# Probabilities transposed one slot later in a fused attention and feed-forward kernel: five probability buffers, latent products in the fifth slot, other engines for the copies

## The chip, the cores and the metric

The kernel runs as one program on one core of a Trainium2 chip. The metric is the time of one execution on the device in microseconds (us). The engines are TensorE (PE in the profile, its weight loads PEld), VectorE (DVE), ScalarE (ACT), GpSimd (POOL) and SyncE (SP), which issues DMAs. Each engine works through its own queue of instructions; semaphores order the queues against one another.

## The reference

The input is 4 sequences of 512 rows of width 512. A block is a feed-forward layer with routed low-rank adapters, then attention, then the same feed-forward layer again. The change is in the attention, which is, cut to what matters:

```python
c_q = x @ w_q_down;  c_kv = x @ w_kv_down;  k_rope = rope(x @ w_k_rope)
q_lat  = einsum('bhsd,hdr->bhsr', q_nope, wuk)          # 32 heads, 64 latent values
scores = einsum('bhsr,btr->bhst', q_lat, c_kv) + einsum('bhsd,btd->bhst', q_rope, k_rope)
probs  = softmax(where(causal, scores / sqrt(192), min))
out_lat = einsum('bhst,btr->bhsr', probs, c_kv)         # the latent products
x = x + (einsum('bhsr,hdr->bhsd', out_lat, wuv) as [s, 4096]) @ w_out
```

## The kernel before

The four sequences are worked one after the other. In the attention of a sequence the 32 heads go in 16 pairs, and the causal score blocks of a pair are dealt to five units, each one PSUM bank of up to 512 columns (`MEMBERS`): units 0 and 1 are the last query block of either head (512 columns), units 2 and 3 are 384 + 128 columns, unit 4 is 256 + 256. So a sequence has 80 slots `u`, with `k = u % 5` the unit and `p = u // 5` the pair, and every engine has a hand-written queue that goes through the slots in this order. `known(g, u, n)` is true from slot n on.

In slot u, TensorE does, in this order: the three score products of unit u (lines L921 to L923, here s0 to s4); in slots k = 0 and 2 the five products that make the queries of one head of the next pair (L906, here q0 and q1); if `k == PV_SLOT`, the latent products of the pair before (`pv`, L957, 20 matmuls); the four transposes of the probabilities of slot `u - T_LAG` (L942, here T0 to T4); and in slots named by `OUT_SLOT`, from slot 15 on, one output row block (`output`, L983, six products).

The softmax of a unit runs over the others. VectorE masks the bank and takes its negated maximum (L1622), ScalarE takes exponentials into one of `RING` buffers `prob` and sums them (L1228), VectorE inverts the sums (L1576, one slot later), GpSimd multiplies (L631). After the transposes, the bank `probT_ps` (two of them, by turns) is copied to `probT` by ScalarE if the unit is in `ACT_BANKS` and else by VectorE (`copy_probT`, L390 and L392). `pv` waits until all five copies of its pair are done (`bank_copies`, with `ACT_COPIES` and `DVE_COPIES` counting them). VectorE also does the rotary part of the queries in slots k = 0 and 2 behind that slot's maximum: one product by the cosines (L1558) and two by the sines (L1563, L1564). It also adds the outputs (L1580) and takes the low part of `oT` (L1629).

Three places in the queues matter. VectorE takes the maximum of slot 3 only behind the rotary part of slot 2. ScalarE's exponential of slot u waits for that slot's maximum. And ScalarE's copy of a bank stands behind the exponential of its slot, except in slot k = 2, where it stands ahead of it:

```python
if copies and k == 2:
    copy_probT(act, nc.scalar, b, g, v)
...            # the exponential of slot u
if copies and k != 2:
    copy_probT(act, nc.scalar, b, g, v)
```

Of the kernel before, what the change touches and what calls it, by code (L numbers as in the profile page):

```python
# [26 lines left out]
F32 = mybir.dt.float32  # L27
# [7 lines left out]
P = 128  # L35
NB, S, D = 4, 512, 512
# [3 lines left out]
QL, KVL, DN, DR, DV = 192, 64, 128, 64, 128  # L40
# [11 lines left out]
STEPS = 3 * ST  # L52
# [17 lines left out]
    ((0, 1, 0), (1, 1, 256)),  # L70
)
RING = 4
T_LAG = 3
PV_SLOT = 3
HEAD_BLOCKS = 11
PT_BLOCKS = 2 * HEAD_BLOCKS
OUT_SLOT = {1: 0, 4: 1}
OUT_SLOT_TAIL = {1: 0, 2: 1}
TAIL = UNITS + 1
ACT_BANKS = (0, 2, 4)  # L80
SLOTS_OUT = 4
ACT_COPIES = (1, 1, 2, 2, 3)
DVE_COPIES = (0, 1, 1, 2, 2)


_INS = ["L0_attn_hidden_states", "L0_attn_w_q_down", "L0_attn_w_q_up_nope", "L0_attn_w_q_up_rope",
# [21 lines left out]
def build(nc, hidden, w_q_down, w_q_up_nope, w_q_up_rope, w_kv_down, w_k_rope, w_uk, w_uv, w_out,  # L108
          W_base, b_base, lora_A, lora_B, router_W, router_b, domain_prior, active,
          rope_cos, rope_sin, rope_cosT, rope_sinT, out):  # L110
    with ExitStack() as ctx:
# [8 lines left out]
        def place(name, shape, dt, at=None):  # L120
            size = int(np.prod(shape[1:])) * mybir.dt.size(dt)
            size = (size + 31) // 32 * 32
            where = cursor if at is None else at
            t = nc.alloc_sbuf_tensor_at(name, list(shape), dt, offset=where[0])
            where[0] += size
            assert where[0] <= sbuf_end, (name, where[0] - sbuf_end)
            return t
# [16 lines left out]
        sin_sb = place("sin_sb", [P, ST, 2, HALF], F32)  # L144
        ident = place("ident", [P, P], F32)
        mask = place("mask", [P, S], F32)
        small = place("small", [P, 60], F32)

        def columns(at, n):
            return small[:, at:at + n]  # L150
# [4 lines left out]
        neg_max = columns(28, 2 * RING).rearrange("p (r m) -> p r m", m=2)  # L155
        row_sum = columns(36, 2 * RING).rearrange("p (r m) -> p r m", m=2)
        inv_sum = columns(44, 2 * RING).rearrange("p (r m) -> p r m", m=2)
        ones, eps, minus_half = columns(52, 2), columns(54, 1), columns(55, 1)
        warm_slot = small[0:1, 56:60]
        region_a = [cursor[0]]  # L160
        wo_hi = place("wo_hi", [P, PAIRS, D], F32R)
        wo_lo = place("wo_lo", [P, PAIRS, D], F32R)
# [12 lines left out]
        rb = [region_b0]  # L175
# [16 lines left out]
        gate_row = place("gate_row", [1, 2 * NE], F32, rb)  # L192
        prior_raw = place("prior_raw", [P, NE], F32, rb)
        bias_nat = place("bias_nat", [P, KC], F32, rb)
        after_staging = rb[0]

        rb = [region_b0]
        prob = [place(f"prob{i}", [P, S], F32, rb) for i in range(RING)]
        probT = place("probT", [P, PT_BLOCKS, P], F32, rb)
        oT_hi = [place(f"oT_hi{i}", [P, S], F32R, rb) for i in range(3)]  # L200
        oT_lo = [place(f"oT_lo{i}", [P, S], F32R, rb) for i in range(3)]
        after_outputs = [rb[0]]
# [3 lines left out]
        moments = place("moments", [P, STEPS, 2], F32, after_outputs)  # L206
        var_eps, rough, newton, rstd = (place(n, [P, STEPS], F32, after_outputs) for n in
                                        ("var_eps", "rough", "newton", "rstd"))
        shift = place("shift", [P, STEPS], F32, [after_outputs[0]])

        uv_nat = [place(f"uv_nat{i}", [P, 2, KVL], F32, after_outputs) for i in range(SLOTS_OUT)]
        cosT = place("cosT", [P, S], F32, after_outputs)
        sinT = place("sinT", [P, S], F32, after_outputs)
        after_scores, turned_home = [after_outputs[0]], [after_outputs[0]]
# [13 lines left out]
        score_ps, probT_ps = X, Z  # L228
# [62 lines left out]
        inv_sum_set, prob_scaled, probT_done = sem("inv_sum_set"), sem("prob_scaled"), sem("probT_done")  # L291
# [55 lines left out]
        def known(g, u, least):  # L347

            return not isinstance(g, int) or BODY * g + u >= least
# [33 lines left out]
        def copy_probT(eng, do, b, g, v):  # L383

            pair = 16 * b + BODY_PAIRS * g + v // UNITS
            eng.wait_ge(probT_done, 80 * b + BODY * g + v + 1)
            if known(g, v, UNITS):
                eng.wait_ge(pv_done, pair)
            if eng.engine == nc.scalar.engine:
                do.activation(probT_unit(v), bank_unit(v), ACT.Copy).then_inc(probT_by_act, 1)  # L390
            else:
                do.tensor_copy(probT_unit(v), bank_unit(v)).then_inc(probT_by_dve, 1)  # L392
# [11 lines left out]
        with nc.Block() as block:  # L404
# [90 lines left out]
            def _(pool):  # L495
# [117 lines left out]
                def attend(b):  # L613
                    def work(g, u):
                        k, p = u % UNITS, u // UNITS
                        if k < 4 and within(g, u, UNITS * LAST_PAIR - 1):
                            m = q_index(b, BODY_PAIRS * g + p + 1, k // 2)
                            if k % 2:
                                qT_low(m, k // 2, (p + 1) % 2)
                            else:  # L620
                                if known(g, u, 1):
                                    pool.wait_ge(prob_scaled, 80 * b + BODY * g + u)
                                else:
                                    pool.wait_ge(qT_lo_set, m)
                                q_sum(m, k // 2, (p + 1) % 2)
                        if within(g, u, SLOTS - 1):
                            n = 80 * b + BODY * g + u
                            pool.wait_ge(inv_sum_set, n + 1)
                            for m, (_, i, c) in enumerate(MEMBERS[u % UNITS]):
                                w = (i + 1) * P  # L630
                                last = nc.gpsimd.tensor_tensor(prob[u % RING][:, c:c + w], prob[u % RING][:, c:c + w],  # L631
                                                               inv_sum[:, u % RING, m:m + 1].broadcast_to([P, w]),
                                                               ALU.mult)
                            last.then_inc(prob_scaled, 1)
                    attention(work, 0)
# [9 lines left out]
            def _(pe):  # L645
# [285 lines left out]
                def transpose_probs(b, g, v):  # L931
                    pe.wait_ge(prob_scaled, 80 * b + BODY * g + v + 1)
                    if known(g, v, 2):
                        by_act, by_dve = bank_copies(b, g, v - 2)
                        if (v - 2) % UNITS in ACT_BANKS:
                            pe.wait_ge(probT_by_act, by_act)
                        else:
                            pe.wait_ge(probT_by_dve, by_dve)
                    for h, i, c in MEMBERS[v % UNITS]:
                        for j in range(i + 1):  # L940
                            at = slice(c + j * P, c + (j + 1) * P)
                            last = nc.tensor.transpose(probT_ps[v % 2][:, at], prob[v % RING][:, at], ident[:])  # L942
                    last.then_inc(probT_done, 1)

                def pv(b, g, p):
# [58 lines left out]
                def attend(b):  # L1004
                    def work(g, u):
# [11 lines left out]
                        if k == PV_SLOT and known(g, u, UNITS):  # L1017
                            pv(b, g, p - 1)
                        if known(g, u, T_LAG) and within(g, u, SLOTS - 1 + T_LAG):
                            transpose_probs(b, g, u - T_LAG)  # L1020
                        if output_rows(u) is not None and known(g, u, 3 * UNITS):
# [12 lines left out]
            def _(act):  # L1034
# [173 lines left out]
                def attend(b):  # L1208
                    def work(g, u):
                        k, p = u % UNITS, u // UNITS  # L1210
                        n1 = BODY_PAIRS * g + p + 1
                        queries = within(g, u, UNITS * LAST_PAIR - 1)
                        if k == 0 and known(g, u, 2 * UNITS):
                            oT_high(b, g, p)
                        if k in (2, 4) and queries:
                            qT_high(q_index(b, n1, k // 2 - 1), k // 2 - 1, (p + 1) % 2)
                        v = u - T_LAG
                        copies = known(g, u, T_LAG) and within(g, u, SLOTS - 1 + T_LAG) and v % UNITS in ACT_BANKS
                        if copies and k == 2:
                            copy_probT(act, nc.scalar, b, g, v)  # L1220
                        if within(g, u, SLOTS - 1):
                            n = 80 * b + BODY * g + u
                            act.wait_ge(neg_max_set, n + 1)
                            if known(g, u, RING):
                                act.wait_ge(probT_done, n - RING + 1)
                            for m, (_, i, c) in enumerate(MEMBERS[k]):
                                w = (i + 1) * P
                                last = nc.scalar.activation(prob[u % RING][:, c:c + w], score_ps[u % 2][:, c:c + w],  # L1228
                                                            ACT.Exp, bias=neg_max[:, u % RING, m:m + 1], scale=-1.0,
                                                            accum_out=row_sum[:, u % RING, m:m + 1])  # L1230
                            last.then_inc(prob_set, 1)
                        if copies and k != 2:
                            copy_probT(act, nc.scalar, b, g, v)
                    attention(work, TAIL)

# [8 lines left out]
            def _(dve):  # L1244
# [363 lines left out]
                def attend(b, more):  # L1608
                    def work(g, u):
# [21 lines left out]
                        if k in (0, 2) and queries:  # L1631
                            if not known(g, u, UNITS):
                                dve.wait_ge(x_moved[k // 2], 32 * b + 1)
                            q_rotary(q_index(b, n1, k // 2), k // 2, (p + 1) % 2, qT_ps[k // 2])
                        v = u - T_LAG
                        if known(g, u, T_LAG) and within(g, u, SLOTS - 1 + T_LAG) and v % UNITS not in ACT_BANKS:
# [34 lines left out]
```

## Time and profile before

| | |
|---|---|
| median of 3 runs | 1167.78 us (1166.98 to 1170.35) |
| profiled execution | 1167.57 us |
| its span, first to last instruction | 1165.8 us |
| busy, share of the span | PE 95%, DVE 78%, POOL 63%, ACT 54% |
| mean granted TensorE clock | 0.992 |

The span is 1.8 us shorter than the time of the same execution. PE's busy time is modelled from pipelined matmuls, so in a list of its instructions the distance from one start to the next is what tells the cost; a duration includes the tail that overlaps the next instruction. A row with an idle time says so in brackets, with what ended it.

### The profile page before, as it was taken

Reading aid. Unit: us, or ns where it says so; the run is one execution under the profiler, and the core shown is the slowest. Engines: PE = TensorE matmul, PEld = TensorE weight load, DVE = VectorE, ACT = ScalarE, POOL = GpSimd, SP = SyncE. Lnnn points to the kernel's source line nnn. Section 1 sums busy time; section 2 is a strip of 40 time slices with the busy share of each in tenths; the row PEclk is TensorE's granted clock in tenths of the full one; section 3 lists DMA queues with packets and bytes.
Section 4 is the critical chain, followed back from the end, with each engine's and each line's share of the span. In section 5 each row is a group of like instructions: output and inputs, shape, how many; then the busy total and the mean of one; then the engine's idle time right before and its main releaser. Section 6 shows DMA issues by size and latency. Waiting matters only on the chain.

```text
span 1165.8 us, 21866 instructions
## 1 busy us (share of the span) xinstructions
PE 1105.7 (95%) x7284; PEld 906.6 (78%) x7284; DVE 908.2 (78%) x2667; ACT 623.9 (54%) x1733; POOL 740.0 (63%) x951
## 2 busy tenths in 40 slices
PE   5896999999998999999999899999999899999997
PEld 4755788888797788888788678888888678888876
DVE  4767888888676888878776888788867787888855
ACT  3554655555454655555535555655545466555542
POOL 2406977887432978787631887787723598877841
PEclk9998999999999999999999999999999999999998
DMA  9660000000101000000101000000010100000000
GB/s 286 179 194 1 1 1 1 1 1 1 37 10 64 2 1 2 1 1 1 37 1 37 37 2 1 2 1 2 1 37 28 47 1 1 1 1 2 1 1 37
DMA packets 22248, 30.96 MB, mean 27 GB/s; under 512 B 9302, under 2 KB 11094, under 8 KB 21498
## 3 DMA queue, kind: packets, MB, share of 16 engines
q1 hardware_dynamic: 19770, 24.85, 6.7%
q10 hardware_dynamic: 2368, 4.72, 1.2%
q8 instruction: 59, 0.97, 0.3%
q14 instruction: 51, 0.42, 0.1%
HBM read 22.23 MB, written 4.19 MB: 23 GB/s over the span
## 4 chain that ended last, share of the span: by engine, by line
PE 79%; DVE 7%; POOL 7%; ACT 3%; issue 2%; SPq 1%; DMA 1%; POOLq 0%; DVEq 0%
PE Y L983 15%; PE Y L957 12%; PE XZ L942 11%; PE Y L906 10%; PE XZ L922 6%; PE XZ L923 6%; PE XZ L921 5%; PE Y L675 4%; POOL prob L631 3%; PE XZ L675 2%; POOL qT_lo L542 2%; PE XZ L650 2%; POOL q_sums L537 2%; DVE xT_lo L1281 1%; ACT xT_hi L1037 1%
## 5 line engine op out<-in xcount | busy, mean ns | idle before, releaser
L1228 ACT ACTIVATE prob<-XZ,small 128x512 f32<-128x512 f32 (+3 forms) x512 | 266.3, 525 | 282.8 <-DVE small L1622 282.8
L631 POOL TENSOR_TENSOR prob<-prob,small 128x512 f32<-128x512 f32 (+3 forms) x512 | 360.7, 721 | 50.1 <-DVE small L1576 40.4
L1622 DVE CUSTOM_DVE_ANT_0 XZ<-XZ,mask 128x512 f32<-128x512 f32 (+3 forms) x512 | 247.9, 506 | 114.6 <-PE XZ L923 110.5
L537 POOL TENSOR_TENSOR q_sums<-q_sums,q_turned 64x512 f32<-64x512 f32 (+2 forms) x130 | 164.2, 1263 | 201.5 <-DVE q_turned L1564 200.1
L942 PE MATMUL XZ<-ident,prob 128*128 128x128 f32 x1280 | 196.3, 276 | 3.2 <-POOL prob L631 2.9
L921 PE MATMUL XZ<-kT_hi,qT_hi 128*128 128x512 f32 (+3 forms) x512 | 176.9, 345 | 12.7 <-ACT prob L1228 6.8
L542 POOL TENSOR_TENSOR qT_lo<-q_sums,qT_hi 128x512 fp32r<-128x512 f32 (+2 forms) x130 | 165.2, 1271 | 31.9 <-ACT qT_hi L1195 31.8
L942 PEld LDWEIGHTS XZ<-ident,prob 128*128 128x128 f32 x1280 | 149.5, 140 | 43.2 <-POOL prob L631 10.6
L922 PE MATMUL XZ<-kT_lo,qT_hi 128*128 128x512 f32 (+3 forms) x512 | 165.4, 323 | 0.0
L923 PE MATMUL XZ<-kT_hi,qT_lo 128*128 128x512 f32 (+3 forms) x512 | 165.2, 323 | 0.0
L957 PE MATMUL Y<-probT,ckv 128*64 128x384 f32 (+2 forms) x1280 | 152.3, 384 | 0.0
L390 ACT ACTIVATE probT<-XZ 128x512 f32<-128x512 f32 x192 | 114.9, 598 | 66.0 <-PE XZ L942 64.8
L957 PEld LDWEIGHTS Y<-probT,ckv 128*64 128x64 f32 x1280 | 81.8, 136 | 60.7 <-issue 47.3
L921 PEld LDWEIGHTS XZ<-kT_hi,qT_hi 128*128 128x128 f32 x512 | 97.2, 190 | 22.8 <-issue 7.7
L983 PE MATMUL Y<-wo_hi,oT_hi 128*128 128x512 f32 x256 | 110.9, 433 | 1.5 <-DVE x_sb L1580 1.4
L1580 DVE TENSOR_TENSOR x_sb<-Y,x_sb 128x512 f32<-128x512 f32 x128 | 87.8, 686 | 29.4 <-PE Y L983 29.1
L1228 ACT ACTIVATION_READ_ACCUMULATOR prob<-XZ,small 128x1 f32 x512 | 101.9, 199 | 0.0
L923 PEld LDWEIGHTS XZ<-kT_hi,qT_lo 128*128 128x128 f32 x512 | 97.3, 190 | 5.5
L922 PEld LDWEIGHTS XZ<-kT_lo,qT_hi 128*128 128x128 f32 x512 | 97.7, 191 | 4.8
L983 PE MATMUL Y<-wo_hi,oT_lo 128*128 128x512 f32 x256 | 101.1, 395 | 0.0
L983 PE MATMUL Y<-wo_lo,oT_hi 128*128 128x512 f32 x256 | 100.2, 391 | 0.0
L1195 ACT ACTIVATE qT_hi<-q_sums 128x512 fp32r<-128x512 f32 (+2 forms) x130 | 80.2, 617 | 19.0 <-POOL q_sums L537 19.0
(220 smaller groups left out, 2162.0 us busy)
## 6 DMA issues: line engine op xcount, KB each, us to landing
wout_nat<-in_L_attn_w_out_dram SPq DMA_DIRECT2D x16, 512.0 KB, 5.0
out_dram<-x_sb SPq DMA_DIRECT2D x16, 256.0 KB, 2.0
x_next<-_attn_hidden_states_dram SPq DMA_DIRECT2D x12, 256.0 KB, 3.4
x_sb<-x_next SPq DMA_DIRECT2D x12, 256.0 KB, 2.3
wbase_nat<-in_L_ffn_W_base_dram ACTq DMA_DIRECT2D x1, 1024.0 KB, 5.7
x_sb<-_attn_hidden_states_dram ACTq DMA_DIRECT2D x4, 256.0 KB, 7.0
nope_a<-_L_attn_w_q_up_nope_dram ACTq DMA_DIRECT2D x1, 1024.0 KB, 5.4
rope_a<-_L_attn_w_q_up_rope_dram SPq DMA_DIRECT2D x1, 1024.0 KB, 8.0
```

The costliest lines, as they stand in the source:

```text
L537: nc.gpsimd.tensor_tensor(q, q, turned, ALU.add).then_inc(q_sum_set, 1)
L542: nc.gpsimd.tensor_tensor(qT_lo[par][:, head, cols], q_sums[par][:, head, cols], f32(qT_hi[par][:, head, cols]), ALU.subtract).then_inc(qT ...
L631: last = nc.gpsimd.tensor_tensor(prob[u % RING][:, c:c + w], prob[u % RING][:, c:c + w], inv_sum[:, u % RING, m:m + 1].broadcast_to([P, w] ...
L906: last = nc.tensor.matmul(bank[:, cols], w, c, start=(j == 0), stop=(j == 4))
L921: nc.tensor.matmul(bank[:, c:c + w], high, kT_hi[:, 0:w], start=True, stop=False)
L922: nc.tensor.matmul(bank[:, c:c + w], high, kT_lo[:, 0:w], start=False, stop=False)
L923: last = nc.tensor.matmul(bank[:, c:c + w], low, kT_hi[:, 0:w], start=False, stop=True)
L942: last = nc.tensor.transpose(probT_ps[v % 2][:, at], prob[v % RING][:, at], ident[:])
L957: last = nc.tensor.matmul(o_ps[64 * h:64 * h + 64, column * P:(column + n) * P], ckv[:, j, :], probT[:, HEAD_BLOCKS * h + at:HEAD_BLOCKS * ...
L983: last = nc.tensor.matmul(bank, o[buffer][:, rows], w, start=(k == 0 and j == 0), stop=(k == 1 and j == 2))
L1228: last = nc.scalar.activation(prob[u % RING][:, c:c + w], score_ps[u % 2][:, c:c + w], ACT.Exp, bias=neg_max[:, u % RING, m:m + 1], scale= ...
L1622: last = nc.vector.tensor_tensor_reduce(bank, bank, mask[:, S - w:S], -1.0, HIGHEST, ALU.add, ALU.min, neg_max[:, u % RING, m:m + 1])
```

## The change

Transposes stand four slots behind the scores instead of three, with a fifth `prob` buffer for it. The latent products move from slot 3 to slot 4, the second output row block from slot 4 to slot 3. ScalarE now copies units 1, 3 and 4, VectorE 0 and 2; each still has as many copies as before, in the same slots. ScalarE's copy stands behind the exponential in every slot. Some small arrays (`shift`, `uv_nat`, constants) get other places in SBUF to make room.

```diff
 RING = 4
-T_LAG = 3
-PV_SLOT = 3
+PROBS = 5
+T_LAG = 4
+PV_SLOT = 4
-OUT_SLOT = {1: 0, 4: 1}
+OUT_SLOT = {1: 0, 3: 1}
 OUT_SLOT_TAIL = {1: 0, 2: 1}
-ACT_BANKS = (0, 2, 4)
+ACT_BANKS = (1, 3, 4)
-ACT_COPIES = (1, 1, 2, 2, 3)
-DVE_COPIES = (0, 1, 1, 2, 2)
+ACT_COPIES = (0, 1, 1, 2, 3)
+DVE_COPIES = (1, 1, 2, 2, 2)
...
-        prob = [place(f"prob{i}", [P, S], F32, rb) for i in range(RING)]
+        prob = [place(f"prob{i}", [P, S], F32, rb) for i in range(PROBS)]
...
-                            last = nc.tensor.transpose(probT_ps[v % 2][:, at], prob[v % RING][:, at], ident[:])
+                            last = nc.tensor.transpose(probT_ps[v % 2][:, at], prob[v % PROBS][:, at], ident[:])
...
                         copies = known(g, u, T_LAG) and within(g, u, SLOTS - 1 + T_LAG) and v % UNITS in ACT_BANKS
-                        if copies and k == 2:
-                            copy_probT(act, nc.scalar, b, g, v)
                         if within(g, u, SLOTS - 1):
                             n = 80 * b + BODY * g + u
                             act.wait_ge(neg_max_set, n + 1)
-                            if known(g, u, RING):
-                                act.wait_ge(probT_done, n - RING + 1)
+                            if known(g, u, PROBS):
+                                act.wait_ge(probT_done, n - PROBS + 1)
...
-                        if copies and k != 2:
+                        if copies:
                             copy_probT(act, nc.scalar, b, g, v)
```

On TensorE, in a pair in the middle of a sequence, these are the rows before, from the transposes T4 of slot 2 through the scores s3 (384 and 128 columns) to the latent products (the number behind a name is that of its buffer):

```order
L942 MATMUL XZ<-ident,prob_104 128x128 x4
L921 MATMUL XZ<-kT_hi,qT_hi_127 128x384
L922 MATMUL XZ<-kT_lo,qT_hi_127 128x384
L923 MATMUL XZ<-kT_hi,qT_lo_129 128x384
L921 MATMUL XZ<-kT_hi,qT_hi_127 128x128
L922 MATMUL XZ<-kT_lo,qT_hi_127 128x128
L923 MATMUL XZ<-kT_hi,qT_lo_129 128x128
L957 MATMUL Y<-probT,ckv 64x384 x2
L957 MATMUL Y<-probT,ckv 64x128 x2
L957 MATMUL Y<-probT,ckv 64x384 x2
```

Only the scores s3 stand between T4 and the latent products that need its copy. Now the same transposes T4 stand in slot 3, behind s3 (of which the last rows are shown), and an output row block and the scores s4 follow:

```order
L923 MATMUL XZ<-kT_hi,qT_lo_129 128x128
L942 MATMUL XZ<-ident,prob_111 128x128 x4
L983 MATMUL Y<-wo_hi,oT_hi_114 128x512
L983 MATMUL Y<-wo_lo,oT_hi_114 128x512
L983 MATMUL Y<-wo_hi,oT_lo_117 128x512
L983 MATMUL Y<-wo_hi,oT_hi_115 128x512
L983 MATMUL Y<-wo_lo,oT_hi_115 128x512
L983 MATMUL Y<-wo_hi,oT_lo_118 128x512
L921 MATMUL XZ<-kT_hi,qT_hi_127 128x256
```

The latent products come behind the six scores of 256 columns, and then T0:

```order
L921 MATMUL XZ<-kT_hi,qT_hi_127 128x256
L922 MATMUL XZ<-kT_lo,qT_hi_127 128x256
L923 MATMUL XZ<-kT_hi,qT_lo_129 128x256
L957 MATMUL Y<-probT,ckv 64x384 x2
L957 MATMUL Y<-probT,ckv 64x128 x2
L957 MATMUL Y<-probT,ckv 64x384 x2
L957 MATMUL Y<-probT,ckv 64x256 x2
L957 MATMUL Y<-probT,ckv 64x128 x2
L942 MATMUL XZ<-ident,prob_107 128x128 x4
```

So one output and one unit of scores more stand between T4 and the latent products, and the same instructions otherwise.

On ScalarE, before, the copy of T4 (the one that writes `probT` as 128x2x2x128) stands ahead of the exponentials of slots 2 and 3:

```order
L1195 ACTIVATE qT_hi_127<-q_sums_133 128x512
L390 ACTIVATE probT<-XZ 128x2x2x128
L1228 ACTIVATE prob_106,small<-XZ,small 128x384
L1228 ACTIVATE prob_106,small<-XZ,small 128x128
L1228 ACTIVATE prob_103,small<-XZ,small 128x384
L1228 ACTIVATE prob_103,small<-XZ,small 128x128
L390 ACTIVATE probT<-XZ 128x4x128
```

Now it stands behind both:

```order
L1195 ACTIVATE qT_hi_127<-q_sums_133 128x512
L1226 ACTIVATE prob_109,small<-XZ,small 128x384
L1226 ACTIVATE prob_109,small<-XZ,small 128x128
L390 ACTIVATE probT<-XZ 128x4x128
L1226 ACTIVATE prob_110,small<-XZ,small 128x384
L1226 ACTIVATE prob_110,small<-XZ,small 128x128
L390 ACTIVATE probT<-XZ 128x2x2x128
L1195 ACTIVATE qT_hi_127<-q_sums_133 128x512
```

What moved: the copy of T4 from ahead of the exponential of slot 2 to behind that of slot 3, and the other two copies name other units.

## Rows read from the trace of the kernel before

**Rows 1.** The page, busy time, share of the span and instructions of each engine:

```profile
PE 1105.7 (95%) x7284; PEld 906.6 (78%) x7284; DVE 908.2 (78%) x2667; ACT 623.9 (54%) x1733; POOL 740.0 (63%) x951
```

**Rows 2.** Windows: length, busy of PE, PEld, DVE, ACT, POOL, granted clock, DMA:

```profile
80.00:96.00 16.00, 10.26 (x59) 6.91 (x57) 10.65 (x31) 5.97 (x17) 4.43 (x5) 0.92 0.03 7
...
370.00:389.00 19.00, 15.19 (x81) 11.58 (x80) 16.91 (x47) 9.74 (x27) 15.43 (x17) 1.00 0.15 56
...
413.00:562.00 149.00, 149.00 (x952) 121.91 (x952) 124.83 (x355) 86.65 (x245) 118.14 (x134) 1.00 0.00 1
```

**Rows 3.** Timeline, TensorE, latent products of sequence 1 (start, us, engine, line):

```profile
389.24 2.38 PE L957 MATMUL Y<-probT,ckv 128*64 128x384 f32 x20
...
413.25 2.38 PE L957 MATMUL Y<-probT,ckv 128*64 128x384 f32 x20
...
561.67 2.38 PE L957 MATMUL Y<-probT,ckv 128*64 128x384 f32 x20
...
583.34 2.38 PE L957 MATMUL Y<-probT,ckv 128*64 128x384 f32 x20
```

**Rows 4.** The transposes by line: what ended TensorE's waits before them:

```profile
  POOL prob L631: 13.5, 31
```

**Rows 5.** Timeline, TensorE, one pair, pv to pv:

```profile
480.71 2.38 PE L957 MATMUL Y<-probT,ckv 128*64 128x384 f32 x20
483.02 0.66 PE L942 MATMUL XZ<-ident,prob 128*128 128x128 f32 x4
483.44 0.36 PE L921 MATMUL XZ<-kT_hi,qT_hi 128*128 128x256 f32 x1
...
484.23 0.60 PE L942 MATMUL XZ<-ident,prob 128*128 128x128 f32 x4
...
486.06 0.39 PE L921 MATMUL XZ<-kT_hi,qT_hi 128*128 128x512 f32 x1
...
488.25 0.48 PE L921 MATMUL XZ<-kT_hi,qT_hi 128*128 128x512 f32 x1
...
489.39 0.47 PE L983 MATMUL Y<-wo_hi,oT_hi 128*128 128x512 f32 x1
...
490.86 0.34 PE L921 MATMUL XZ<-kT_hi,qT_hi 128*128 128x384 f32 x1
...
492.87 0.60 PE L942 MATMUL XZ<-ident,prob 128*128 128x128 f32 x4
493.22 0.42 PE L921 MATMUL XZ<-kT_hi,qT_hi 128*128 128x384 f32 x1
...
494.21 2.38 PE L957 MATMUL Y<-probT,ckv 128*64 128x384 f32 x20
```

**Rows 6.** Timeline, ScalarE, the same pair: copy of T4; copy behind exponential of slot 3:

```profile
480.01 0.60 ACT L390 ACTIVATE probT<-XZ 128x512 f32<-128x512 f32 x1 [1.02 <-PE XZ L942]
...
483.72 0.60 ACT L390 ACTIVATE probT<-XZ 128x512 f32<-128x512 f32 x1
```

**Rows 7.** Timeline, VectorE, the same pair: maxima of slots 3, 0, 3, rotary part between:

```profile
481.75 0.57 DVE L1622 CUSTOM_DVE_ANT_0 XZ<-XZ,mask 128x384 f32<-128x384 f32 x1
...
486.94 0.70 DVE L1622 CUSTOM_DVE_ANT_0 XZ<-XZ,mask 128x512 f32<-128x512 f32 x1
...
493.13 0.67 DVE L1558 TENSOR_TENSOR q_sums<-Y,cosT 128x512 f32<-128x512 f32 x1
...
495.25 0.57 DVE L1622 CUSTOM_DVE_ANT_0 XZ<-XZ,mask 128x384 f32<-128x384 f32 x1
```

**Rows 8.** Timeline, VectorE, second and third pair of sequence 1:

```profile
388.11 0.69 DVE L1558 TENSOR_TENSOR q_sums<-Y,cosT 128x512 f32<-128x512 f32 x1
...
394.35 0.69 DVE L1622 CUSTOM_DVE_ANT_0 XZ<-XZ,mask 128x512 f32<-128x512 f32 x1
...
395.41 0.69 DVE L1629 TENSOR_TENSOR oT_lo<-Y,oT_hi 128x512 fp32r<-128x512 f32 x1 [0.29 <-ACT oT_hi L1206]
...
400.32 0.68 DVE L1558 TENSOR_TENSOR q_sums<-Y,cosT 128x512 f32<-128x512 f32 x1
```

More of the change, by code:

```diff
@@ L146, in build @@
         mask = place("mask", [P, S], F32)
-        small = place("small", [P, 60], F32)
+        small = place("small", [P, 64], F32)
         def columns(at, n):
@@ L157, in build @@
         inv_sum = columns(44, 2 * RING).rearrange("p (r m) -> p r m", m=2)
-        ones, eps, minus_half = columns(52, 2), columns(54, 1), columns(55, 1)
-        warm_slot = small[0:1, 56:60]
+        ones, eps, minus_half, warm_slot = columns(5, 2), columns(3, 1), columns(4, 1), small[0:1, 2:3]
+        shift = columns(52, STEPS)
         region_a = [cursor[0]]
@@ L194, in build @@
         bias_nat = place("bias_nat", [P, KC], F32, rb)
+        uv_nat = [place(f"uv_nat{i}", [P, 2, KVL], F32, rb) for i in range(SLOTS_OUT)]
         after_staging = rb[0]
         rb = [region_b0]
-        prob = [place(f"prob{i}", [P, S], F32, rb) for i in range(RING)]
+        prob = [place(f"prob{i}", [P, S], F32, rb) for i in range(PROBS)]
         probT = place("probT", [P, PT_BLOCKS, P], F32, rb)
@@ L208, in build @@
                                         ("var_eps", "rough", "newton", "rstd"))
-        shift = place("shift", [P, STEPS], F32, [after_outputs[0]])
-        uv_nat = [place(f"uv_nat{i}", [P, 2, KVL], F32, after_outputs) for i in range(SLOTS_OUT)]
         cosT = place("cosT", [P, S], F32, after_outputs)
@@ L630, in work @@
                                 w = (i + 1) * P
-                                last = nc.gpsimd.tensor_tensor(prob[u % RING][:, c:c + w], prob[u % RING][:, c:c + w],
+                                last = nc.gpsimd.tensor_tensor(prob[u % PROBS][:, c:c + w], prob[u % PROBS][:, c:c + w],
                                                                inv_sum[:, u % RING, m:m + 1].broadcast_to([P, w]),
@@ L1223, in work @@
                             act.wait_ge(neg_max_set, n + 1)
-                            if known(g, u, RING):
-                                act.wait_ge(probT_done, n - RING + 1)
+                            if known(g, u, PROBS):
+                                act.wait_ge(probT_done, n - PROBS + 1)
                             for m, (_, i, c) in enumerate(MEMBERS[k]):
                                 w = (i + 1) * P
-                                last = nc.scalar.activation(prob[u % RING][:, c:c + w], score_ps[u % 2][:, c:c + w],
+                                last = nc.scalar.activation(prob[u % PROBS][:, c:c + w], score_ps[u % 2][:, c:c + w],
                                                             ACT.Exp, bias=neg_max[:, u % RING, m:m + 1], scale=-1.0,
```

## The prediction

> **What bounds the kernel now.** I read the page first: TensorE is busy 95% of the span, no other engine above 78% [rows 1]. Then the windows by stage: in the even part of the attention of sequence 1 (413 to 562 us) TensorE is busy 149.00 of 149.00 us at the full granted clock of 2.4 GHz, while VectorE has 24 us to spare in it [rows 2]. The list of latent products (pv) says the same more sharply: from the third to the fourteenth of sequence 1 there are 11 periods in 561.67 - 413.25 = 148.42 us, 13.49 us each [rows 3]. A pair costs what its matmuls cost, and nobody is waited for. Only the head and the tail of an attention have gaps. All waits of TensorE for scaled probabilities, which are what a longer lag can take away, are 13.5 us in the whole kernel [rows 4].
>
> So in the even part the change can win nearly nothing: the same matmuls come in another order. What has to be asked is whether a new wait arises, and for that I follow the one wait that was placed anew, that of pv for the copy of T4, the last transposes of its pair.
>
> **How much time TensorE leaves.** Times below count from Q, the start of the transposes right behind q1; in the pair shown Q is 492.87. Before, T4 stands at Q itself and pv comes 494.21 - 492.87 = 1.34 us later [rows 5]. The copy of T4 fits in only because ScalarE does it ahead of its exponentials: it ends at 480.01 + 0.60 = 480.61, and pv starts at 480.71, 0.10 later [rows 5, 6]. After the change TensorE has from Q: T3 (493.22 - 492.87 = 0.35), s3 (494.21 - 493.22 = 0.99), T4 (0.35), an output (490.86 - 489.39 = 1.47), s4 (484.23 - 483.44 = 0.79) [rows 5]. It reaches pv at Q + 3.95. That is 2.6 us more room than before, but the copy has moved too.
>
> **How much the copy needs.** It now stands on ScalarE behind the exponential of slot 3, which waits for the maximum of slot 3, which stands on VectorE behind the rotary part of q1. From rows: the rotary part starts at 493.13, Q + 0.26; the maximum of slot 3 at 495.25, which is 2.12 after it; and ScalarE comes to the copy behind the exponential 483.72 - 481.75 = 1.97 us after that maximum starts [rows 6, 7]. The copy takes 0.60 and pv follows 0.10 later, as before. Together Q + 0.26 + 2.12 + 1.97 + 0.60 + 0.10 = Q + 5.05. pv is 5.05 - 3.95 = 1.10 us late. Behind it in TensorE's queue stand T0 and the scores, query products and outputs of the next pair. They lead to the next Q, so the delay isn't caught up: it comes again with every pair.
>
> The Trainium skill (TensorE: Matmul & The Clock Gate, the row on engine queue depth) says that ScalarE and VectorE are strict FIFO and that TensorE can only pull weight loads ahead. By that rule no instruction slips past the exponential. A case in which the copy overtakes it would have no stall and is priced below, with the rivals.
>
> **The new period.** It is the loop from pv to pv. pv to T0 takes 483.02 - 480.71 = 2.31 and T0 0.42; then s0 starts, at pv + 2.73. The maximum of s0 comes 486.94 - 486.06 = 0.88 after its start, and 0.09 more because a score group behind transposes is that much longer (0.48 against 0.39): pv + 3.70. From there VectorE works without a gap to the rotary part of q1: 493.13 - 486.94 = 6.19, so pv + 9.89 [rows 5, 7]. (TensorE gets to Q at pv + 2.73 + 0.09 + (492.87 - 486.06) = 9.63, and Q + 0.26 is the same 9.89: both limits agree.) Then 2.12 + 1.97 + 0.60 + 0.10 = 4.79 to the next pv. The period is 14.68 us, 1.19 more than 13.49. The unknown is how the pieces of VectorE's work pack together once it has waited: at least 4.79 + 9.63 + 0.1 = 14.5, at most the 14.68 with another 0.2 for a copy of T0 that comes late, 14.9. I take 14.68, since every term has its own row.
>
> **Sum for a sequence.**
> - The 11 even periods and the one ahead of them are full ones with both outputs: 12 x 14.68 = 176.2.
> - Between the first and second pv no output is worked. VectorE needed 400.32 - 394.35 = 5.97 from the maximum of s0 to the rotary part, of which 0.29 was a wait for ScalarE's `oT_hi`, which then comes in time since pv ends earlier against s0 [rows 8]; 3.70 + 5.67 + 4.79 = 14.2.
> - So first to fourteenth pv takes 190.4 against 561.67 - 389.24 = 172.4 before [rows 3]: +18.0.
> - The first pv: the rotary part of the second pair started at 388.11 with VectorE as the limit, so it stays there, and pv comes 4.79 later, at 392.9 instead of 389.24 [rows 3, 8]: +3.7. The scores s4 that now stand ahead of pv are within this.
> - The last two pv: the last pair has no query products, so VectorE isn't held and I count 0.3 of stall before the fifteenth. In the tail an output (1.47) and a score group (0.79) have moved ahead of that pv, while a copy of 0.6 that lay under an output is bare, as are some 0.6 for the banks: -1.0. Together -0.7 against the 21.67 between the fourteenth and the last pv [rows 3]; bounds -1.5 and +1.
>
> That is +21.0 for a sequence and +84 for four; the opening and the mixed steps between attentions keep their instructions. Against the profiled execution's 1167.57 us (0.2 below the median, so I correct nothing) it gives 1251.6 us, 7.2% slower.
>
> The lighter work of VectorE in slot 4 (the added output moves to slot 3), the fifth buffer and the longer lag are costed at nothing. They relax waits that in the even part nobody has: the transposes follow the matmul ahead of them at once [rows 5]. If their cover were gone they would be worth at most the 13.5 us of rows 4. The moved arrays change no instruction's size. No DMA moves in its queue: the loads of the next sequence still wait for the last scores.
>
> **Rivals.**
> 1. *The new order pays and nothing stalls.* pv would find its copy done if the path to it were shorter by 1.10 us, so from the point at which the copy ended before Q + 3.85. It would then save, at most, the 13.5 us of rows 4 and 0.09 a pair by which s3 ahead of pv may have been held by its copy, 5.4 us over some 60 pairs: 1167.6 - 18.9 = 1149 us; with little of it, 1160. For it speaks that before the copy was only 0.10 us ahead [rows 5, 6]. Against it speaks the order on ScalarE. 0.05.
> 2. *No stall and no gain,* since TensorE was full before and is full after: 1167 us, within 0.3%. Needs the same condition. 0.03.
> 3. *A smaller stall.* If the pairs without outputs and the head lose only the 1.2 us each that full pairs lose, instead of 3.7, 2.6 and 2.3, a sequence loses 5 less and the time is about 1231; with a period of 14.5 as well, 1223. Same mechanism, 0.20.
> 4. *The clock falls as well.* TensorE now pauses 1.1 us in every pair. In the opening, with TensorE busy 10.26 of 16 us, the granted clock was 0.92; with 15.19 of 19 us it was 1.00 [rows 2]. A pair would be busy 92%, above both, so I expect the full clock. At 0.92 the 9.63 us from pv to Q would be 10.47, 0.84 more, of which some 0.8 reach pv: with 12 or 13 such pairs in each of 4 sequences about +40, 1290 us. The Trainium skill (same page, on a second failure mode of the gate) describes a kernel in which short pauses between groups of matmuls made the clock swing; the 1.00 in the head here, with its gaps, is against that. 0.04.
> 5. *The forecast:* a stall of 1.0 to 1.4 in every pair, 1240 to 1265 us. 0.68.
>
> **How the numbers follow.** 1251.6 us is the likeliest case. The range takes cases 5 and 3, from 1223 to 1268, the upper end being a period of 14.8 and no gain in the tail. What a measurement of this kernel can tell from no change is about 0.3%, 3.5 us. Faster by more is case 1, 0.05; within it case 2, 0.03; slower cases 3 to 5, 0.92.
>
> **What the new profile would show.** pv to pv about 14.7 us in every middle pair. ScalarE's copy of T4 directly behind the exponential of slot 3, ending 0.1 us before pv. Ahead of pv a wait of TensorE of about 1.1 us, with ScalarE's copy (now a line near L390) as its releaser, some 55 to 65 us in the whole kernel, and more in the early pairs. VectorE in slot 4 idle until T0 is done. I am wrong if pv to pv stays at 13.5, if the wait stands in front of something else, or if the granted clock in the even part is below 1.00.

## The result and the profile after

The changed kernel takes 1254.22 us (median of 4 runs, 1253.16 to 1255.6), the kernel before 1168.07 us on the same chip (1166.98 to 1170.35): 1.0735 times as long, 95% interval 1.0714 to 1.0757. The profiled execution's span is 1251.1 us, 85.3 more than the 1165.8 before. The prediction said 1251.6, between 1223 and 1268.

The page after: busy time by engine, and the shares of the chain that ended last.

```profile
PE 1118.9 (89%) x7284; PEld 910.7 (73%) x7284; DVE 911.6 (73%) x2667; ACT 621.3 (50%) x1733; POOL 741.3 (59%) x951
...
DVE 49%; PE 34%; ACT 9%; issue 6%; POOL 1%; SPq 1%; DMA 1%; ACTq 0%; DVEq 0%; POOLq 0%
```

The instruction counts are those of [rows 1], and the busy times of all engines but TensorE are within 0.5% of them. TensorE's grew by 13.2 us, which its clock explains in part, below. What changed is what the end waits for: the chain now runs mostly over VectorE, half of its length, where before TensorE had 79% of it.

The table of waits after (engine, line, waited for: us in total, times, longest us):

```profile
DVE probT L392 <- PE XZ L942: 192.9, 64, 6.0
PE Y L957 <- ACT probT L390: 69.0, 60, 2.5
```

The second line is the forecast stall: the latent products wait in 60 of 64 pairs for ScalarE's copy, 69.0 us. The first shows VectorE idle, at the same place in every pair, for the transposes T0 behind those products. A sum of 192.9 us looks like the larger trouble, but nothing is lost there that the second line has not already lost: T0 stands behind pv on TensorE, and run 1, in which T0 stands behind pv as well, has its period back.

The timeline after, TensorE, latent products of sequence 1 (answers to [rows 3]; start, us, engine, line, and in brackets the wait and its releaser):

```profile
417.06 3.82 PE L957 MATMUL Y<-probT,ckv 128*64 128x384 f32 x20 [2.50 <-ACT probT L390]
...
432.64 2.38 PE L957 MATMUL Y<-probT,ckv 128*64 128x384 f32 x20 [2.51 <-ACT probT L390]
...
447.18 2.38 PE L957 MATMUL Y<-probT,ckv 128*64 128x384 f32 x20 [0.98 <-ACT probT L390]
...
505.34 2.38 PE L957 MATMUL Y<-probT,ckv 128*64 128x384 f32 x20 [0.99 <-ACT probT L390]
...
519.87 2.38 PE L957 MATMUL Y<-probT,ckv 128*64 128x384 f32 x20 [0.98 <-ACT probT L390]
...
607.12 2.38 PE L957 MATMUL Y<-probT,ckv 128*64 128x384 f32 x20 [0.98 <-ACT probT L390]
```

A middle period is 519.87 - 505.34 = 14.53 us (14.54 over all of them) against 13.49, with a wait of 0.98 in each. The first two pv wait 2.5 us, and the first takes 3.82 us itself instead of 2.38. The pair in between, on each of the three engines (answers to [rows 5 to 7]): TensorE first.

```profile
514.95 0.60 PE L942 MATMUL XZ<-ident,prob 128*128 128x128 f32 x4
...
516.20 0.62 PE L942 MATMUL XZ<-ident,prob 128*128 128x128 f32 x4
...
518.61 0.28 PE L923 MATMUL XZ<-kT_hi,qT_lo 128*128 128x256 f32 x1
```

Then VectorE and ScalarE in the same pair:

```profile
515.22 0.67 DVE L1556 TENSOR_TENSOR q_sums<-Y,cosT 128x512 f32<-128x512 f32 x1
...
517.33 0.57 DVE L1620 CUSTOM_DVE_ANT_0 XZ<-XZ,mask 128x384 f32<-128x384 f32 x1
...
522.88 0.69 DVE L392 COPY probT<-XZ 128x512 f32<-128x512 f32 x1 [3.06 <-PE XZ L942]
```
```profile
518.31 0.58 ACT L1226 ACTIVATE prob<-XZ,small 128x384 f32<-128x384 f32 x1 [1.48 <-DVE small L1620]
...
519.23 0.59 ACT L390 ACTIVATE probT<-XZ 128x512 f32<-128x512 f32 x1
```

Read it as a chain. Q is 514.95. T4 stands at 516.20 and is done at 516.82. From 516.83 on ScalarE, which could copy it, sits idle for 1.48 us at the exponential of slot 3. That waits for the maximum at 517.33, and that stands behind the rotary part of 515.22. The exponentials end, the copy starts at 519.23, pv at 519.87. TensorE had come to pv at 518.89.

Where the 85.3 us are, over the four sequences, with start-to-start distances of pv from the timelines of both kernels:

| stretch | before | after | sum of 4 | predicted |
|---|---|---|---|---|
| to the first pv (added delay) | | +3.63, +4.60, +3.19, +2.30 | +13.7 | +14.8 |
| first to second pv | 11.58 | 15.57 | +16.0 | +10.5 |
| second to third | 12.43 | 17.32, 14.54, 15.93, 14.54 | +12.6 | +9.0 |
| 11 middle periods | 13.49 | 14.54 | +46.0 | +52.4 |
| last two | 21.67 | 20.92 | -3.0 | -2.8 |

The heads cost more than predicted, the steady part less. The granted clock tells why of the heads (windows after, in sequence 1: us, busy of PE, PEld, DVE, ACT, POOL, clock, DMA):

```profile
414.00:417.00 3.00, 0.56 (x5) 0.35 (x4) 2.37 (x11) 1.52 (x7) 2.84 (x3) 1.00 0.00 0
417.00:421.00 4.00, 3.94 (x21) 2.10 (x22) 0.00 (x0) 1.51 (x7) 3.00 (x5) 0.60 0.00 0
...
434.00:607.00 173.00, 161.39 (x1024) 131.09 (x1020) 135.80 (x384) 91.25 (x261) 127.00 (x144) 1.00 0.00 1
```

TensorE pauses 2.5 us, and in the pv behind it the clock is 0.60, mostly at its lower level of 1.2 GHz; T0 starts 3.75 us after pv instead of 2.31. The four first pv are all slowed in this way, of the four second pv two. In the middle, with a pause of 0.98 in every pair, it is 1.00.

### The profile page after: what moved, and what is told of

It reads as the page before. It is cut to its first block, busy times and chain, and to the rows that moved or that the text cites. A ratio compares the mean times of both kernels' runs of the same rounds, so it can differ in the third digit from the quotient of the medians.

```text
span 1251.1 us, 21862 instructions
## 1 busy us (share of the span) xinstructions
PE 1118.9 (89%) x7284; PEld 910.7 (73%) x7284; DVE 911.6 (73%) x2667; ACT 621.3 (50%) x1733; POOL 741.3 (59%) x951
## 4 chain that ended last, share of the span: by engine, by line
DVE 49%; PE 34%; ACT 9%; issue 6%; POOL 1%; SPq 1%; DMA 1%; ACTq 0%; DVEq 0%; POOLq 0%
DVE XZ L1620 13%; PE Y L957 13%; DVE q_turned L1562 7%; DVE q_sums L1556 6%; DVE probT L392 6%; DVE q_turned L1561 5%; PE XZ L942 4%; ACT prob L1226 3%; PE Y L675 3%; PE Y L983 3%; DVE x_sb L1578 3%; ACT probT L390 3%; DVE oT_lo L1627 2%; PE XZ L675 2%; DVE small L1620 2%
## 5 line engine op out<-in xcount | busy, mean ns | idle before, releaser
L392 DVE COPY probT<-XZ 128x512 f32<-128x512 f32 x128 | 87.3, 682 | 192.9 <-PE XZ L942 192.9
L957 PE MATMUL Y<-probT,ckv 128*64 128x384 f32 (+2 forms) x1280 | 161.1, 401 | 69.3 <-ACT probT L390 69.0
L957 PEld LDWEIGHTS Y<-probT,ckv 128*64 128x64 f32 x1280 | 85.4, 142 | 141.7 <-ACT probT L390 82.2
```

The source lines that it names most:

```text
L957: last = nc.tensor.matmul(o_ps[64 * h:64 * h + 64, column * P:(column + n) * P], ckv[:, j, :], probT[:, HEAD_BLOCKS * h + at:HEAD_BLOCKS * ...
```

## The experiments

My theory: the copy of T4 is ready to run but held in ScalarE's queue behind the exponential of slot 3, which VectorE's rotary part holds. Rivals: the longer lag itself costs (banks or buffers come free later), or the clock does. Beside each run stands a run of the kernel before on the same chips (1167.87, 1169.46 and 1169.49 us for runs 1 to 4, 5 to 6, 7 to 8).

**1. The copy ahead of the exponential** (change to the kernel after):

```diff
+                        if copies and k == 3:
+                            copy_probT(act, nc.scalar, b, g, v)
                         ...            # the exponential of slot u
-                        if copies:
+                        if copies and k != 3:
                             copy_probT(act, nc.scalar, b, g, v)
```

> The changed kernel with one thing given back: ScalarE's copy of T4 stands ahead of the exponential of slot 3. Theory (pv waits for this copy, which waits for the exponential, which waits for VectorE's rotary part): the copy is done near Q + 2.5, TensorE comes to pv at Q + 3.9, no wait. pv to pv falls from 14.54 to 13.4 to 13.5 us, the whole to 1162 to 1172 us. Rival (the fourth slot of lag itself starves VectorE, whose copy of T0 waits 3 us behind pv): the period stays above 14.2 and the whole above 1230.

Measured 1177.56 us (1177.19 to 1177.89), ratio to before 1.0085 (1.0068 to 1.0102). Timeline of this run, TensorE, and what is left of the wait:

```profile
432.05 2.38 PE L957 MATMUL Y<-probT,ckv 128*64 128x384 f32 x20
...
445.57 2.38 PE L957 MATMUL Y<-probT,ckv 128*64 128x384 f32 x20
...
459.09 2.38 PE L957 MATMUL Y<-probT,ckv 128*64 128x384 f32 x20
```
```profile
PE Y L957 <- ACT probT L390: 2.7, 4, 0.7
```

No bracket, and a period of 13.52 us: one copy put ahead of one exponential takes back 76.7 of the 86.2 us. The middle of the kernel is TensorE's again. So the longer lag and the fifth buffer cost at most 0.03 us a period there, and they bring nothing: the period isn't under 13.49. Yet the run missed its expectation by 6 us at the upper side. Of the 9.5 us left in the span (1175.3), 8.5 are in the delay to the first pv (0.95, 3.16, 3.10, 1.27), 4.2 between the second and third (13.47 instead of 12.43: two outputs now stand there instead of one), 1.2 in the middle; 3.7 come back in the last pair and 0.7 in smaller pieces. Part of the delay to the first pv is clock: it is 0.66 here,

```profile
375.00:380.00 5.00, 4.98 (x19) 4.43 (x19) 3.54 (x12) 2.21 (x7) 3.28 (x3) 0.66 0.28 105
```

where before it was 1.00 from 370 to 389 [rows 2], though TensorE's instructions and its pauses up to there (0.78, 1.25 and 0.74 us) are the same in both. It is not this run alone: the same three pauses stand in the openings of sequences 1 to 3 (counted from 0) in this run and in both kernels. At them the clock falls in all three here, in one of the kernel after and in one of the kernel before. The kernel after in sequence 1, then the kernel before in sequence 3:

```profile
397.00:401.00 4.00, 3.97 (x13) 3.49 (x14) 3.21 (x11) 1.44 (x4) 2.29 (x3) 0.57 0.35 131
```
```profile
919.00:923.00 4.00, 3.25 (x11) 2.85 (x11) 2.94 (x6) 0.73 (x4) 2.26 (x3) 0.57 0.41 154
```

From the last pv of a sequence to the first of the next it is 78.8 us before where the clock stays up and 79.64 where it falls, 82.0 and 83.39 after, 80.91 with one fall in this run and 81.91 and 81.95 with two, the second behind a pause of 2.39 us. By these differences, and that is an estimate, about 0.7 us of the delay in each of sequences 1 to 3 is left without the clock, so that some 5 of the 9.5 us are clock. What decides whether it falls is open.

**2. The same order in the old schedule** (change to the kernel before: the copy in slot 2 goes behind its exponential, the lag stays at three):

```diff
-                        if copies and k == 2:
-                            copy_probT(act, nc.scalar, b, g, v)
...
-                        if copies and k != 2:
+                        if copies:
```

> The kernel before with one thing taken: ScalarE's copy of T4 in slot 2 stands behind the exponential of that slot instead of ahead. Lag 3, pv in slot 3, hands as before. Theory: loop pv to s0 5.35, to its maximum 0.88, to the maximum of slot 2 5.39, its exponential 0.90 + 0.98, the copy 0.60, 0.05 to pv: 14.15 a pair against 13.49, whole 1205 to 1222 us. Rival (lag and slots cost it): within 5 us of the kernel before.

Measured 1209.87 us (1209.36 to 1210.8), ratio 1.036 (1.0343 to 1.0378). Its timeline:

```profile
442.39 2.38 PE L957 MATMUL Y<-probT,ckv 128*64 128x384 f32 x20 [0.50 <-ACT probT L390]
...
456.47 2.38 PE L957 MATMUL Y<-probT,ckv 128*64 128x384 f32 x20 [0.50 <-ACT probT L390]
```

The period is 14.07, 0.58 more than 13.49, near the 14.15 expected. The order alone, with nothing else of the change, costs 42 us. It costs less than in the kernel after; here the maximum of slot 2 is what the copy hangs on, there that of slot 3. In one place this run has a slow pv too, the second of sequence 0, though TensorE has paused only 0.59 and then 1.08 us ahead of it:

```profile
129.90 4.07 PE L957 MATMUL Y<-probT,ckv 128*64 128x384 f32 x20 [1.08 <-ACT probT L390]
```
```profile
129.90:133.90 4.00, 4.00 (x21) 2.00 (x21) 1.36 (x6) 1.02 (x4) 3.35 (x4) 0.57 0.00 0
```

In the other three sequences the same two pauses, 0.58 and 1.10 us, are followed by a pv of 2.38.

**3. The copy of T4 in VectorE's hands** (change to the kernel after, with the ring of `inv_sum` as long as `PROBS`, and that array repacked):

```diff
-ACT_BANKS = (1, 3, 4)
+ACT_BANKS = (0, 1, 3)
-ACT_COPIES = (0, 1, 1, 2, 3)
-DVE_COPIES = (1, 1, 2, 2, 2)
+ACT_COPIES = (1, 2, 2, 3, 3)
+DVE_COPIES = (0, 0, 1, 1, 2)
```

> The changed kernel with unit 4 copied by VectorE in slot 3 and units 0, 1, 3 by ScalarE; the inverted sums get five places instead of four, since VectorE no longer waits for T0. Theory: VectorE is done with the maximum and the inversion at Q + 3.30, copies 0.67, pv at Q + 4.02 against the 3.88 at which TensorE gets there: 0.15 of wait, 13.65 a pair; early pairs without outputs lose about 1.5 each: 1178 to 1195 us. Rival (any hand is as late): no faster than 1245.

Measured 1203.11 us (1199.02 to 1207.44), ratio 1.0304 (1.0268 to 1.0339). The middle period is 13.65, as expected, but the total is 8 us above the range. The loss moved to the ends. In the last pair of a sequence the copy stands behind the next sequence's statistics on VectorE, in this run's timeline:

```profile
596.49 1.41 DVE L1247 BATCH_NORM_STATS2 stats<-x_next 128x6 f32<-128x512 f32 x2
...
600.07 0.68 DVE L392 COPY probT<-XZ 128x512 f32<-128x512 f32 x1
```

The last two pv are then 10.75 apart instead of 9.42 (9.62 in the last sequence, which has no next); the first two are 13.05 apart instead of 11.43 in run 1, and from the last pv of a sequence to the first of the next it is 84.23 to 84.32, in run 1 80.91 to 81.95. Part of that last difference is clock: TensorE pauses 2.1 us ahead of the last pv of sequences 0 to 2, and it takes 4.06, 3.89 and 3.75 us.

```profile
600.84 3.89 PE L957 MATMUL Y<-probT,ckv 128*64 128x384 f32 x20 [2.13 <-issue]
```
```profile
600.80:604.80 4.00, 3.96 (x21) 2.41 (x21) 0.82 (x5) 0.03 (x1) 0.15 (x1) 0.59 0.00 0
```

The stall in the middle doesn't belong to ScalarE as such: another hand that is free by then removes most of it.

**4. Work put back over the stall** (change to the kernel after: the second output stands in slot 4, behind pv, no longer ahead of it):

```diff
-OUT_SLOT = {1: 0, 3: 1}
+OUT_SLOT = {1: 0, 4: 1}
```

> The changed kernel with the second output row block back in slot 4, where it stands behind pv and T0. Theory: the wait at pv ends at the same time after Q, and the 1.47 us of output are now in the part from pv to Q: the period grows by 1.47 to 16.0, the wait to 2.4 us, the whole by 65 to 1319 us. If a pause of 2.5 us ahead of pv takes TensorE's clock down, as it does ahead of the first pv of each sequence in the changed kernel, each pv costs 1.4 more and the whole comes to some 1380 us. Rival (outputs are as good in either slot): 1254.

Measured 1383.64 us (1382.39 to 1385.21), ratio 1.1849 (1.1828 to 1.1869). Timeline, then windows of this run:

```profile
496.50 3.98 PE L957 MATMUL Y<-probT,ckv 128*64 128x384 f32 x20 [2.34 <-ACT probT L390]
...
514.02 2.38 PE L957 MATMUL Y<-probT,ckv 128*64 128x384 f32 x20 [2.33 <-ACT probT L390]
...
547.51 4.07 PE L957 MATMUL Y<-probT,ckv 128*64 128x384 f32 x20 [2.33 <-ACT probT L390]
```
```profile
440.00:680.00 240.00, 206.39 (x1206) 160.46 (x1205) 159.78 (x458) 110.24 (x315) 150.72 (x171) 0.92 0.00 1
547.50:551.00 3.50, 3.49 (x16) 1.73 (x18) 0.00 (x0) 1.38 (x5) 2.52 (x4) 0.51 0.00 0
```

The pause is 2.33 where 2.4 was expected: the output of 1.47 us had covered that much of the wait. And the second price, the clock, comes on top: after some of these pauses pv takes 4.0 us and the period is 17.3 to 17.6, after others 2.38 and 15.92. This run decides between its two expectations for the one with the falling clock.

**5. The rotary part of the second head one slot later** (change to the kernel after):

```diff
-                        if k in (0, 2) and queries:
+                        if k in (0, 3) and within(g, u - k, UNITS * LAST_PAIR - 1):
...
-                            q_rotary(q_index(b, n1, k // 2), k // 2, (p + 1) % 2, qT_ps[k // 2])
+                            q_rotary(q_index(b, n1, k // 3), k // 3, (p + 1) % 2, qT_ps[k // 3])
```

> The changed kernel with VectorE's rotary part of the second head in slot 3, behind the maximum and the inversion of that slot, instead of in slot 2. ScalarE's order is as in the changed kernel. Theory (the rotary part is the long link of the chain): the maximum of slot 3 starts at Q + 1.5, the exponential ends at 3.4, the copy at 4.0, pv at Q + 4.1 against 3.9 for TensorE: a wait of 0.2, 13.7 a pair, 1175 to 1195 us. Rival (only ScalarE's order matters): no change, 1254.

Measured 1190.94 us (1190.15 to 1193.73), ratio 1.0185 (1.0152 to 1.0218). Waits and timeline of this run:

```profile
PE Y L957 <- ACT probT L390: 10.7, 12, 1.3
PE XZ L921 <- POOL qT_lo L542: 14.3, 10, 3.3
```
```profile
453.43 2.38 PE L957 MATMUL Y<-probT,ckv 128*64 128x384 f32 x20
...
466.96 2.38 PE L957 MATMUL Y<-probT,ckv 128*64 128x384 f32 x20
```

With ScalarE's order left as it is and only its releaser moved, the wait falls from 69.0 to 10.7 us and the period to 13.54. That is the upper half of the chain, shown by itself. Part of the price has moved: the queries of some early pairs now come late (14.3 us in 10 waits, against 5.5 in 4 in the kernel after).

**6 and 7. Keeping TensorE at work in the first two pauses.** Twenty transposes of the identity, into a bank that pv overwrites right after, stand ahead of the wait in the first two pairs of a sequence. In run 6 the wait for `oT` had come ahead of that for the copies in all pairs as well; run 7 leaves the order as it was in the other pairs.

```diff
+                    filled = g == 0 and p < 2
+                    if filled:
+                        ...            # the waits for oT_hi and oT_lo, which read the same bank
+                        for _ in range(20):
+                            nc.tensor.transpose(o_ps[:, 0:P], ident[:], ident[:])
                     pe.wait_ge(probT_by_act, by_act)
                     pe.wait_ge(probT_by_dve, by_dve)
-                    if known(g, UNITS * p, UNITS):
+                    if known(g, UNITS * p, UNITS) and not filled:
```

> The changed kernel with 20 transposes of the identity into the output bank of pv, ahead of TensorE's wait for the copies, in the first two pairs of each sequence only. They take 1.8 us of a wait of 2.5 and are overwritten. Theory (the pause takes the clock down and the first latent products of a sequence run at half of it): these pv take 2.3 instead of 3.8 us, first to second pv 14.1 instead of 15.6, the whole 1242 to 1249 us. Rival (the slow pv has another cause): 1254, or more by the filler.

> The filler of e6_filler again (20 transposes of the identity ahead of the wait for the copies, first two pairs of each sequence), but in all other pairs the four waits of pv stand in the order of the changed kernel: copies first, output halves last. Theory (the pause takes the clock down ahead of the first pv; e6_filler lost what it won to the order of the waits): middle pairs 14.54 again, first to second pv about 14.0, the whole 1242 to 1250 us. Rival (the filler costs what it wins): 1254.

Run 6: 1256.84 us (1256.05 to 1258.56), ratio 1.0743 (1.071 to 1.0777), a miss. Run 7: 1244.89 us (1244.35 to 1245.02), ratio 1.0637 (1.0601 to 1.0673). First run 7's timeline and a window of it, then run 6's timeline in the middle, ScalarE and TensorE:

```profile
427.90 2.38 PE L964 MATMUL Y<-probT,ckv 128*64 128x384 f32 x20 [0.32 <-ACT probT L390]
...
442.44 2.38 PE L964 MATMUL Y<-probT,ckv 128*64 128x384 f32 x20 [0.99 <-ACT probT L390]
```
```profile
427.90:432.00 4.10, 4.10 (x30) 2.86 (x31) 1.09 (x2) 1.98 (x6) 2.96 (x5) 1.00 0.00 0
```
```profile
504.50 0.59 ACT L390 ACTIVATE probT<-XZ 128x512 f32<-128x512 f32 x1
...
505.35 2.38 PE L960 MATMUL Y<-probT,ckv 128*64 128x384 f32 x20 [1.18 <-ACT probT L390]
```

In run 7 all pv take 2.38, the first two are 13.95 apart instead of 15.57, the second and third 14.54 in all sequences, and the span is 1243.0, 8.1 less: 10.7 won in the heads, 2.8 lost on the way to the first pv. Added work on the engine that waits made the kernel faster: that part of the loss was the clock and not the wait. In run 6 the heads gain the same, but each middle period is 14.74 instead of 14.54, from 0.85 instead of 0.64 us between the start of the copy and pv.

**8. The order of pv's four waits alone** (change to the kernel after):

```diff
-                    pe.wait_ge(probT_by_act, by_act)
-                    pe.wait_ge(probT_by_dve, by_dve)
                     ...            # the waits for oT_hi and oT_lo
+                    pe.wait_ge(probT_by_act, by_act)
+                    pe.wait_ge(probT_by_dve, by_dve)
```

> The changed kernel with nothing but the order of pv's four waits turned: output halves first, copies last, so that the wait that really ends last also stands last. Theory: the time from the start of ScalarE's copy to pv is 0.85 us as in e6_filler instead of 0.64, the period 14.74, the whole 1260 to 1268 us. Rival (in e6_filler the early filler pairs shift everything after them): 14.54 and 1254.

Measured 1273.95 us (1272.51 to 1275.53), ratio 1.0885 (1.0847 to 1.0924). Timeline of this run:

```profile
434.81 4.53 PE L957 MATMUL Y<-probT,ckv 128*64 128x384 f32 x20 [2.71 <-ACT probT L390]
...
481.71 2.38 PE L957 MATMUL Y<-probT,ckv 128*64 128x384 f32 x20 [1.20 <-ACT probT L390]
```

The middle period is 14.74, as in run 6: the order of the waits is what run 6 lost. The copies' waits stand third and fourth here; ScalarE's, which ends last, is the third and not, as the expectation says, the last. The total is 6 us above the range. The pause ahead of the second pv has grown from 2.51 to 2.71, and behind it that pv is now slow in all four sequences (second to third 16.37 to 17.49), where in the kernel after it was in two.

No run was faster than the kernel before; the best form of the change, run 1, is 0.85% slower, part of it by the clock.

## Why the prediction was right

**The bound before.** Right: run 1 takes the stall away and the period goes back to 13.52. In an even part in which TensorE is full [rows 2] the longer lag won nothing. The 13.5 us of rows 4, read as TensorE's waits, are 2.9 of its products and 10.6 of its weight loads, so even the small gain that rival 1 was priced at was priced high.

**Time that TensorE leaves.** Q + 3.95 was forecast; measured 518.89 - 514.95 = 3.94.

**Time that the copy needs.** Rotary part at Q + 0.26: measured 0.27. From it to the maximum 2.12: measured 2.11. From the maximum to the copy 1.97: measured 1.90. The copy and the way to pv 0.70: measured 0.64. The stall is 0.98 instead of 1.10. The term 1.97 was read before from a copy of T0 [rows 6] that had its own transposes to wait for until 483.68, so 0.07 of it was not the exponentials'. The 0.10 between the end of the copy and pv came from a pair in which the releaser I named need not have been the last thing pv hung on.

**The period.** 14.68 forecast, 14.54 measured, at the lower bound of 14.5 that was given: 0.13 of it are the two terms above. Over 44 middle periods that is 6.4 us too much. The waits of pv are 69.0 us in the whole, 47 of them in the 48 pairs from the third to the fourteenth and 19 in the first two; 55 to 65 were forecast and "more in the early pairs".

**That the loop doesn't catch up.** Right: every middle pair waits, with the same 0.98. That it is this loop is shown by cutting it at two places: on ScalarE (run 1, 13.52) and on VectorE (run 5, 13.54). Run 3, another hand, 13.65, and run 2, the order alone, 14.07, agree.

**Strict order of the queues.** No instruction of ScalarE slipped past the exponential, on which it sat 1.48 us with the copy ready; so the rule of the Trainium skill that the prediction weighed (TensorE: Matmul & The Clock Gate, engine queue depth) held.

**The heads.** First pv +3.7 a sequence: measured +3.63, +4.60, +3.19, +2.30. The +4.60 has a fall of the clock in the kernel after, the +2.30 one in the kernel before (the two windows at run 1); in sequence 2, where it stays up in both, the delay is 3.19, so the term was some 0.5 too dear. First to second 14.2: measured 15.57, and run 7 gives 13.95 with the clock kept up. So the mechanism was priced within 0.25 and the clock was left out. Rival 4 was priced for middle pairs and given 0.04. It came true in the heads only. Against run 7 the clock cost 4 x 1.62 from the first to the second pv and 17.32 - 14.54 = 2.78 and 15.93 - 14.54 = 1.39 behind the second, together 10.7 us. The step that failed is "a pair would be busy 92%, so I expect the full clock". I had asked for the busy share of a pair and not for the length of the single pause, though the stall of the first pairs was known to be longer than that of the others. And the 1.00 of [rows 2] that spoke against rival 4 was that of sequence 1; in the opening of sequence 3 the kernel before itself had 0.57.

**The tail.** -0.7 a sequence forecast, -0.75 measured (11.50 and 9.42 instead of 11.32 and 10.35).

**The range.** Its upper end doesn't follow from its words: a period of 14.8 in 48 periods and no gain in the tail add 5.8 and 2.8 us to 1251.6 and give 1260, not 1268. The measured time lies below either.

The total of 1251.6 against 1254.22 is closer than its terms deserve, and that is luck: the steady part was some 6 us too dear, the heads about 9 us too cheap, the first pv 1 us too dear.

## What to carry to other kernels

When a wait is moved in a software pipeline, follow what is ahead of its producer in the producer's own queue, not only how much work lies between producer and consumer: here 2.6 us more room were bought, and the copy came 3.64 us later (it starts at Q + 4.28 instead of Q + 0.64). Where a copy's input is ready early, it belongs ahead of an instruction that waits for another engine. And if the stalled engine is TensorE, price the pauses as well as the busy share, since the work behind a pause of 2 us, and at times behind two or three of about 1 us close together, may run at half the clock.

## What the runs showed of the hardware

- The clock fell behind many pauses of 2.1 to 2.7 us: to 0.60 at 417 to 421 us after, to 0.51 in run 4 (pv 4.07 instead of 2.38), to 0.59 in run 3 behind 2.13 us. But the same 2.33 us in run 4, and the same 2.51 ahead of the second pv after, were at times followed by the full clock.
- It also fell behind shorter pauses that stood close together: behind 0.59 and 1.08 us in run 2 (0.57, pv 4.07), and at a group of 0.78, 1.25 and 0.75 us in the openings, in the kernel before too (0.57 at 919 to 923 us). The same groups of pauses were followed by the full clock in other sequences. It never fell behind the one pause of 0.98 in each middle period after. So the length of a pause doesn't decide alone; what does is open. The Trainium skill (TensorE: Matmul & The Clock Gate, on a second failure mode of the gate) describes a clock that swings with short pauses between groups of matmuls; run 4, with 0.92 over 240 us, agrees with it, and the middle of the kernel after, with 1.00, doesn't agree.
- With transposes of the identity in the pause the clock stayed up: in run 7 it was 1.00 in every pv of the heads, and these took 2.38.
- With four waits ahead of one instruction, having the one that ends last stand third cost 0.20 us more than having it stand first (runs 6 and 8: 14.74 against 14.54 a period). I would have guessed the reverse, since waits that are long satisfied could have been worked off under it. Why is open.
